# Node stages of a four-layer graph network: sums and inner rows in PSUM, GpSimd's additions behind VectorE's, another order of the slots

## What is computed

```
x = _layernorm(x + _L0_gnn_ref(x, ...))   # edge MLP, mean over a node's edges, node MLP, inner layernorm
x = _layernorm(x + _L1_gnn_ref(x, ...))   # attention with self loops, + x @ skip_W + biases, inner layernorm
x = _layernorm(x + _L2_gnn_ref(x, ...))   # attention, 8 heads' layout of 16 columns, no inner norm
x = _layernorm(x + _L3_gnn_ref(x, ...))   # attention, batch norm, relu, x + h
```

## Time and profile before

| | us |
|---|---|
| median of 3 runs | 8903.67 |
| lowest and highest run | 8887.96, 8942.08 |
| the profiled execution | 8913.7 |
| its span | 8911.7 |
| VectorE busy | 5056.9 |
| TensorE busy | 6934.7 |
| GpSimd busy | 6300.6 |

### The profile page before, as it was taken

One profiled execution on the slowest core, in us unless ns is written; L12 is line 12 of the kernel. 1 busy time (PEld: TensorE's weight loads), 2 busy tenths in 40 slices (PEclk: granted clock), 3 DMA queues, 4 the chain that ended last, 5 costly groups with the idle time before them and its releaser, 6 DMA issues.

```text
span 8911.7 us, 139091 instructions
## 1 busy us (share of the span) xinstructions
PE 6934.7 (78%) x41513; PEld 5837.6 (66%) x41514; DVE 5056.9 (57%) x12625; ACT 2080.3 (23%) x7255; POOL 6300.6 (71%) x6607
## 2 busy tenths in 40 slices
PE   6999999998777777777747777777766777777775
PEld 5777777776566666666636666666655666666664
DVE  3333333334766666666686666666666666666666
ACT  2222222222322222222222222222212222222222
POOL 4777777775677777777657777777765777777774
PEclk8999889998888888887768888888877888888886
DMA  3333333332222222222222222222222222222221
GB/s 100 80 78 80 76 76 77 80 78 64 73 66 66 66 66 66 67 67 66 64 70 69 69 69 69 68 70 69 69 64 66 68 69 69 68 70 69 69 69 49
DMA packets 425472, 625.66 MB, mean 70 GB/s; under 512 B 189634, under 2 KB 305617, under 8 KB 425293
## 3 DMA queue, kind: packets, MB, share of 16 engines
q0 software_dynamic: 206336, 462.61, 21.3%
q1 hardware_dynamic: 219086, 162.49, 7.1%
HBM read 598.03 MB, written 26.58 MB: 70 GB/s over the span
## 4 chain that ended last, share of the span: by engine, by line
PE 37%; POOL 26%; issue 17%; DVE 12%; DVEq 4%; DMA 2%; SPq 1%; ACT 1%; POOLq 0%; ACTq 0%
POOL G L559 25%; PE ps L708 11%; PE ps L755 8%; PE ps L730 6%; PE ps L725 6%; DVEq L1216 3%; DVE msg L1335 3%; PE ps L698 2%; DVE acc L1242 2%; DMA G<-rows,idx 2%; PE ps L776 1%; DVE acc L1232 1%; DVE shared L1289 1%; DVE shared L1297 1%; PE ps L786 1%
## 5 line engine op out<-in xcount | busy, mean ns | idle before, releaser
L559 POOL DMA_INDIRECT G<-rows,idx x6448 | 6127.0, 950 | 2197.1 <-issue 1914.3
L1162 DVE TENSOR_TENSOR memb<-rel,ps 128x1664 f32<-128x1664 f32 x496 | 936.3, 1888 | 1828.2 <-PE ps L708 1827.9
L708 PE MATMUL ps<-msg,memb 128*128 128x136 f32 (+2 forms) x12896 | 1733.7, 295 | 128.0 <-DVE msg L1335 125.5
L755 PE MATMUL ps<-membT,shared 128*104 128x128 f32 x9672 | 1772.0, 356 | 2.2 <-ACT membT L919 2.2
L708 PEld LDWEIGHTS ps<-msg,memb 128*128 128x128 f32 x12896 | 1655.6, 203 | 156.2 <-issue 87.7
L755 PEld LDWEIGHTS ps<-membT,shared 128*104 128x104 f32 x9672 | 1605.5, 236 | 24.7 <-issue 3.0
L698 PE MATMUL ps<-ident,memb 128*128 128x128 f32 x6448 | 1092.9, 312 | 462.6 <-DVE memb L1162 420.6
L1242 DVE TENSOR_TENSOR acc<-acc,ps 128x136 f32 (+2 forms) x3472 | 1023.8, 295 | 421.4 <-DVE acc L1242 346.3
L698 PEld LDWEIGHTS ps<-ident,memb 128*128 128x128 f32 x6448 | 792.5, 155 | 679.8 <-issue 362.9
L919 ACT ACTIVATE membT<-ps 128x512 f32<-128x512 f32 x1984 | 952.2, 504 | 77.6 <-PE ps L698 66.5
L1335 DVE TENSOR_TENSOR msg<-G,ps 128x1768 f32<-128x1768 f32 x372 | 742.7, 1996 | 242.6 <-PE ps L786 238.5
(11 more groups left out here) (179 smaller groups left out, 4627.6 us busy)
## 6 DMA issues: line engine op xcount, KB each, us to landing
G<-rows,idx POOLq DMA_INDIRECT x6448
shared<-marks_all SPq DMA_DIRECT2D x372, 156.0 KB
shared<-in_edge_attr SPq DMA_DIRECT2D x124, 256.0 KB
shared<-in_edge_attr SPq DMA_DIRECT2D x124, 160.0 KB
rows<-msg SPq DMA_DIRECT2D x36, 288.0 KB, 2.8
idx<-in_src SPq DMA_DIRECT2D x496, 6.5 KB
xrows<-msg SPq DMA_DIRECT2D x24, 256.0 KB, 2.2
memb<-xrows SPq DMA_DIRECT2D x24, 256.0 KB, 3.0
```

Source lines behind the costliest of these rows:

```text
L559: nc.gpsimd.indirect_dma_start(G[:, b, t, 0:rows[l].shape[1]], None, rows[l], bass.IndirectOffsetOnAxis(idx[:, b, t:t + 1], 0)).then_inc(g ...
L708: last = mm(ps_sum[k // 2][:, 0:width], memb[:, b, k * P:(k + 1) * P], msg[:, b, k, 0:width], start=k % 2 == 0, stop=k % 2 == 1 or k == K - 1)
L755: last = mm(ps_sc[b][0:JH, :], adz[:, k // 2, K - 1 - k:K - 1 - k + JH], membT[:, k, :], start=k == 0, stop=False)
L1162: tt(memb[:, b, :].rearrange("p (k n) -> p k n", k=K), r, w, ALU.is_equal).then_inc(memb_ready, 1)
```

## The change

- PSUM banks are used in the node stages for three things: the weighed sums of stages 1 and 2 (`n_weighed`, banks 0 and 1), the inner rows (`n_y_rows`, banks 6 and 7) and, in the last loop, the relu rows (`f_relu_rows`, banks 4 and 5). `s_y` is gone.
- `addends` is split. `base_rows(t+1)` stands between `power(1, t-1)` and `power(0, t)`; `residual_rows(t+1)` stands after them and waits, for blocks from 2 on, for `n_agg`, the sums of block t+2.
- In stage 1 the row of biases `reps[3]` is added by TensorE (four more matmuls a block with one-row weights) and not by GpSimd; the own rows times their shares remain on GpSimd.
- In stage 0 the bias product `b2_u1` of the hidden rows comes last of the three.
- In stage 2 VectorE's slot is another: residual, table of block t-2, shifts of block t, sums of block t+1.

```diff
-        s_r, s_y, s_t = (ring(gflat, 2 * k * BLK, 2) for k in range(3))
+        s_r, s_t = (ring(gflat, 2 * k * BLK, 2) for k in range(2))
+        n_weighed, n_y_rows, f_relu_rows = ps[:, 0:2, :], ps[:, 6:8, :], ps[:, 4:6, :]
...
-            def addends(l, s):
+            def base_rows(l, s):
                 pool.wait_ge(x_in[x], 16 * (ring_uses(g, 3) + 1))
                 if s >= 2:
                     pool.wait_ge(n_var[0], g - 1)
...
-                    nc.gpsimd.tensor_tensor(base, base, rep(3), ALU.add).then_inc(n_base, 1)
+
+            def residual_rows(l, s):
+                g = NS * l + s
+                n, x = QN[s], g % 3
+                if s >= 2:
+                    pool.wait_ge(n_agg, NS * l + min(s + 2, NS))
                 if s >= 3:
                     pool.wait_ge(n_var[1], g - 2)
-                nc.gpsimd.tensor_tensor(xb, xr, rep(4 + l), ALU.add).then_inc(n_xb, 1)
+                nc.gpsimd.tensor_tensor(rowsof(s_xb[:, x, 0:n * P]), rowsof(s_x[:, x, 0:n * P]),
+                                        reps[:, 4 + l, :].unsqueeze(1).to_broadcast([P, n, P]), ALU.add).then_inc(n_xb, 1)
...
                 mm(n_hidden[:, 0:n], u1[:, 0, :], xT[:, d], start=True, stop=False)
+                pe.wait_ge(n_aggT_in, s + 1)
+                mm(n_hidden[:, 0:n], w2u[:, :], s_agg[:, s % 2, 0:n], start=False, stop=False)
                 if s == 0:
                     pe.wait_ge(n_some_row, 32)
-                mm(n_hidden[:, 0:n], b2_u1[0:1, :], some_row[0:1, d], start=False, stop=False)
-                pe.wait_ge(n_aggT_in, s + 1)
-                mm(n_hidden[:, 0:n], w2u[:, :], s_agg[:, s % 2, 0:n], start=False, stop=True).then_inc(n_hid_out, 1)
+                mm(n_hidden[:, 0:n], b2_u1[0:1, :], some_row[0:1, d], start=False, stop=True).then_inc(n_hid_out, 1)
...
-                        last = mm(n_update[:, f], xT[:, s * BLK + q * P:s * BLK + (q + 1) * P], wsk[:, :],
-                                  start=True, stop=True)
+                        mm(n_update[:, f], xT[:, s * BLK + q * P:s * BLK + (q + 1) * P], wsk[:, :],
+                           start=True, stop=False)
+                        last = mm(n_update[:, f], ones[0:1, :], reps[0:1, 3, :], start=False, stop=True)
...
-                normalise(s_y[:, g % 2, :], s_r[:, g % 2, :], 0, g % 2, QN[s], n_y)
+                normalise(n_y_rows[:, g % 2, :], s_r[:, g % 2, :], 0, g % 2, QN[s], n_y)
...
-                then(weighed(both_halves(s, 0, MW), shares(1, s)))
+                g = NS + s
+                weighed(both_halves(s, 0, MW), shares(1, s), wide(n_weighed[:, g % 2, 0:QN[s] * P], QN[s])).then_inc(n_agg, 1)
...
-                    then(tt(wide(d, n), wide(d, n), of_heads(even(s, 0, MW)), ALU.add))
+                    dve.wait_ge(n_agg, g + 1)
+                    then(tt(d, d, n_weighed[:, r, 0:n * P], ALU.add))
...
-                if s >= 2:
-                    dve.wait_ge(n_xnew, g - 1)
-                then(weighed(both_halves(s, 0, MW), weights_of(s), wide(s_t[:, g % 2, 0:QN[s] * P], QN[s])))
+                weighed(both_halves(s, 0, MW), weights_of(s), wide(n_weighed[:, g % 2, 0:QN[s] * P], QN[s])).then_inc(n_agg, 1)
...
-                    stt(s_t[:, s % 2, 0:n], xT[:, cols_of(s)], 2.0, s_y[:, s % 2, 0:n], ALU.mult,
+                    stt(s_t[:, s % 2, 0:n], xT[:, cols_of(s)], 2.0, f_relu_rows[:, s % 2, 0:n], ALU.mult,
```

More of the change, by code:

```diff
@@ L583, in addends @@
                 if l == 0:
-                    nc.gpsimd.tensor_tensor(base, xr, rep(2), ALU.add).then_inc(n_base, 1)
+                    nc.gpsimd.tensor_tensor(rowsof(s_base[:, g % 2, 0:n * P]), rowsof(s_x[:, x, 0:n * P]),
+                                            reps[:, 2, :].unsqueeze(1).to_broadcast([P, n, P]), ALU.add).then_inc(n_base, 1)
                 else:
@@ L608, in node_stage @@
                 for t in SLOTS:
[L609 to L615, removed]
+                    s = at(t, 1)
+                    if s is not None and l < 2:
+                        power(1, l, s)
+                    s = at(t, -1)
+                    if s is not None and l < 2:
+                        base_rows(l, s)
                     s = at(t, 0)
                     if s is not None:
-                        power(1, l, s)
+                        power(0 if l < 2 else 1, l, s)
+                    s = at(t, -1)
+                    if s is not None and l < 2:
+                        residual_rows(l, s)
             for l in range(4):
@@ L1524, in node_stage @@
                     s = at(t, 0)
[L1525 to L1538 removed]
+                    g = NS * l + t
+                    if l < 2:
+                        if s is not None:
+                            update(l, s)
+                        s = at(t, 1)
+                        if s is not None:
+                            shifts(1, (g - 1) % 2, QN[s], n_rstd[1], g, n_shift[1])
+                        s = at(t, 3)
+                        if s is not None:
+                            table(l, s)
+                        s = at(t, 0)
+                        if s is not None:
+                            shifts(0, g % 2, QN[s], n_rstd[0], g + 1, n_shift[0])
+                        s = at(t, -2)
+                        if s is not None:
+                            (means, shared_sums)[l](s)
+                        s = at(t, 0)
+                        if s is not None:
+                            residual(l, s)
+                    else:
+                        if s is not None:
+                            residual(l, s)
+                        s = at(t, 2)
+                        if s is not None:
+                            table(l, s)
+                        s = at(t, 0)
+                        if s is not None:
+                            shifts(1, g % 2, QN[s], n_rstd[1], g + 1, n_shift[1])
                         s = at(t, -1)
@@ L1541, in node_stage @@
                             value_sums(s)
-                    else:
-                        s = at(t, -2)
-                        if s is not None:
-                            (means, shared_sums)[l](s)
-                    s = at(t, 0)
-                    if s is not None:
-                        residual(l, s)
             for l in range(4):
```

46 lines of the change are left out of this document (12 added, 34 removed).

## The result

| | before | after |
|---|---|---|
| median of 9 runs each, us | 8923.5 | 8847.7 |
| lowest and highest run, us | 8888.0, 8942.1 | 8817.1, 8879.8 |
| ratio, 95% interval | | 0.9928, 0.991 to 0.9946 |
| the profiled execution, us | 8913.7 | 8858.5 |

The change saves 76 us: 0.85% between the medians, 0.7% by the ratio, whose interval excludes no change. The median of the nine runs of before stands 20 us above that of the first three, on which the forecast was built, so its difference (73 us) is the better measure of it than its level (8831).

The account below looks back on a forecast made before the run. GpSimd's gathers fill the untouched sweeps; VectorE's queue bounds stages 0 and 1, a round trip stage 2. Gains 22.3 + 27.8 + 21 + 1.5 = 73 us, from 8903.7 to 8831 us, range 8797 to 8877.

Parts of the forecast that it names:

- The level: Whole kernel: 8831 us after the change, against 8903.7, the median of the first three runs.
- The stop of two SBUF inputs against a GpSimd addition: Stages 0 and 1: each waits for the other's end, costing 1.06 + 0.97 us per slot of stage 0.
- Stage 0: First node stage: 22.3 us less, with slots of 8.6 us and a start 2.0 us earlier.
- Stage 1: Second node stage: 27.8 us less, slots falling from 12.00 to 9.2 us.
- The bias on TensorE: Stage 1: four more one-row matmuls a block, at most 2.08 us more, costed at 0 because covered.
- Stage 2: Third node stage: 21 us less, slots falling from 7.41 to 5.65 us.
- PSUM as an operand: All node stages: about 104 VectorE passes read or write PSUM, at 0 us extra each.
- slower: Rival, chance 0.03: PSUM makes VectorE's passes longer; 0.7 us more on each of 104 cancels the gain.
- The last loop: After the last sweep: power falls from 1.39 to 1.01 us; 1.5 us gained (0 to 4.5).
- One input is held too: Rival, chance 0.07: GpSimd additions also hold VectorE passes with one SBUF input; 30 us gained, kernel at 8874.
- TensorE bounds stage 0: Rival, chance 0.12: TensorE's 7.7 us per slot grow at a lower clock; kernel at 8843 or 8869.
- More: Rival, chance 0.10: TensorE's clock grant rises and stages' last slots shrink, some 5 us a stage; 8816.

Follow-up runs that it names:

- e1: Changed kernel with the inner rows of stages 0 and 1 and stage 2's sums back in SBUF: slots of 9.47, 10.18 and 5.72 us.
- e2: Kernel before, its orders kept, with inner rows and stage 2's sums in PSUM, those sums without their wait: stages of 152.1, 174.3 and 89.0 us.
- e3: Changed kernel without the residual addition's wait for the sums: slots of 9.4 to 9.8 us in stage 0, 10.17 in stage 1.
- e6: Changed kernel with all GpSimd additions of stages 0 and 1 behind the sums: stages of 128.8, 143.5 and 81.9 us; ratio to before 0.9911.
- e4: Changed kernel with stage 1's bias on GpSimd again and stage 0's hidden products in old order: slots of 9.72 us in stage 1, 8.52 in stage 0.
- e5: Changed kernel with stage 1's sums and the last loop's rows in SBUF, stage 2's table a slot later: slots 9.12 and 5.73, stage 2 85.2 us.
- e7: The changed kernel unaltered, run once more: ratio to before 0.99; stages of 129.4, 146.1 and 83.3 us, 82.5 behind the last sweep.

## Why the prediction was right, point by point

**The whole.** Forecast: 73 us less. Measured: 73.9 in the edited parts, 76 between the medians. The parts were off by up to 1.7 us, and these errors cancelled in the sum. The level, 8831, was 17 us low, about as much as the median of the first three runs of before lay below that of all nine (20).

**The stop of two SBUF inputs against a GpSimd addition.** This was the core, and e1, e2 and e3 show it from three sides: a stop of 0.95 to 1.06 us appears when either the operand or the place is put back. The rule of the Trainium skill's page "SBUF — State Buffer", section "Who interferes with whom", fits: of the passes of 128x512 with one SBUF input, 47 ran beside a GpSimd addition or multiplication in stages 0 and 1 of after, and all took 0.69 to 0.70 us.

**Stage 0: 22.3 forecast, 20.6 measured.** The full slots gave 1.96 us each (1.9 forecast); the 0.2 us for the small pass held by the base addition was forecast at 0.13, and e6 took it back. The start gave 2.3 (2.0 forecast). TensorE's last hidden product has only this left behind the wait of the earlier trace rows:

```profile
2196.83 1.92 PE L816 MATMUL ps<-shared,w2u 128*128 128x512 f32 x2
2201.22 1.12 PE L819 MATMUL ps<-shared,b_u 1*128 1x512 f32 x2 [2.48 <-DMA shared<-flags]
```

Two terms were mis-sized. Slot 10 gave 0.9 and not 2.0: its short sums no longer cover ScalarE's inner rows, the very thing that I took off in stage 1's slot 10 and forgot here.

```profile
2296.91 0.70 DVE L1485 TENSOR_TENSOR ps<-ps,reps 128x512 f32<-128x512 f32 x1 [0.93 <-ACT ps L1000]
```

And the end, from the last update on, took 12.6 us instead of 11.1. There TensorE's products follow one another with nothing to hide them, and eight of L854 took 1.30 us in before at 2306.42, at 2.4 GHz, but 2.39 in after, at 1.2 GHz. The change isn't shown to be the cause: e2, with the orders of before, has 2.39 and an end of 12.4 too, and e3, with those of after, 1.30 and 11.3.

```profile
2314.39 2.39 PE L854 MATMUL ps<-wext,xT 128*128 128x152 f32 x8 [0.69 <-ACT xT L919]
```

**Stage 1: 27.8 forecast, 29.1 measured.** Slots of 9.11 (9.2 forecast); the full ones gave 2.89 each, slot 0 1.1 (0.6), slot 10 1.8 (1.9). The bias on TensorE, costed at 0, cost 0, but its price was mis-sized. I had put it at "at most 2.08 more" for an update. At the same granted clock of 0.50 the eight products of before took 2.08 us and the sixteen of after 5.86, which is 3.78 more:

```profile
4528.53 0.80 PE L832 MATMUL ps<-wsk,xT 128*128 128x128 f32 x2 [2.62 <-DVE varn L1370]
...
4533.60 0.79 PE L834 MATMUL ps<-reps,ones 1*128 1x128 f32 x2
...
4534.66 0.69 DVE L1471 TENSOR_TENSOR G<-ps,memb 128x512 f32<-128x512 f32 x1
```

They end 0.26 us before the update that reads them. So it is, within 0.01, in seven of slots 1 to 9; in the other two the clock was higher and 2.5 us are left. Slot 10 leaves 0.14. TensorE was busy for 105 us of 146, 8.1 a slot and not 7.3 (60 of 175 in before), though in ten full slots it still sat idle for 22 us waiting for VectorE. So the 0 held by a narrow margin, and by luck as far as the argument goes; a slot of stage 1 much shorter than 9.11 would meet TensorE at this clock. That the row on TensorE was necessary (0.61 a slot, e4) wasn't in the sum; I had counted only the stops that it removed.

**Stage 2: 21 forecast, 21.1 measured, by other parts.** Slots of 5.73 against 5.65, and the full slots gave 1.7 each, ten of them where I had counted eleven. I overlooked that before the change made two blocks' sums ahead of the first residual and after makes one: the first residual comes 2.1 us earlier, and those sums fall into slot 10, which gave only 0.46 us. The stage's end gave 1.8; I had put the earlier table at 0.7, and e5 gives 3.0 for it at the same clock. The errors cancelled, which is luck. And the cause was half misread: PSUM for stage 2's sums, which I made a part of the gain, is worth nothing once the order is changed (e1), because by then ScalarE has long read `s_t`.

**PSUM as an operand: 0 forecast.** L1485, in place in PSUM, 0.69; L1487 0.69; L1446 writing into PSUM 0.70 against 0.69 into SBUF. None of these passes took even 1.1 times its former length, so the rival "slower" had nothing to stand on. The 65 ns a pass that the Trainium skill's page "VectorE: DVE Perf Modes", section "The TRN2 errata", would give for a source in PSUM are not in the traces.

**The last loop: 1.5 forecast, 3.1 measured.** The power takes 1.01 there (1.39 before); some 0.25 us of the 0.38 came through in each of twelve blocks.

**The rivals.** "One input is held too": L1485 and L1487 beside a full addition show no stop. "TensorE bounds stage 0": in after it still waits for VectorE in each slot, at a granted clock of 0.79 for the stage:

```profile
2252.42 1.12 PE L819 MATMUL ps<-shared,b_u 1*128 1x512 f32 x2
2254.61 0.66 PE L806 MATMUL ps<-ident,acc 128*128 128x128 f32 x4 [1.07 <-DVE acc L1457]
```

In e7 it came close. There every second slot of the later ones took 8.74 us, and at the end of each of these VectorE waited 0.15 us for TensorE's update product, the sign that the prediction had named for this rival:

```profile
2237.67 0.69 DVE L1471 TENSOR_TENSOR G<-ps,memb 128x512 f32<-128x512 f32 x1 [0.15 <-PE ps L830]
```

The slots between them took 8.32, so that the mean stayed at 8.53. "More": the clock's grant didn't rise (0.79, 0.54 and 0.57 against 0.77, 0.57 and 0.58 between the same bounds), and the ends of stages 0 (after against before) and 2 (e7 against after) took 1.5 us more where eight products ran at 1.2 GHz. The sweeps, which the argument left out, moved by 17 us, over three times the errors of its four parts added up without their signs (4.7).

## What to carry to other kernels

Look for small VectorE passes that take about as long as a GpSimd instruction beside them: here a 0.16 us pass took 1.22. Such a stop needs both an operand and a place: in stage 0 moving the second operand to PSUM gave nothing, moving the GpSimd work half, the two together all, so each addition was put behind a semaphore at the place where VectorE reads PSUM. Compare stages and slots rather than whole times when a change is under 1%: single executions of the same sweep code differed by 50 us in the first sweep alone, while nearly all full slots of stages 1 and 2 repeated within 0.03 us. Those of stage 0 varied by 0.4 us, though their mean stayed at 8.5.

## What the runs showed of the hardware

A small pass with one SBUF input can be held as well: L1370 (one input of 128x4, two constants) takes 0.17 us, 0.37 where a GpSimd addition still runs, and 0.78 in e4; in each case it ends with the addition. Row statistics with one input beside the same additions keep their 0.87 and 0.38 us. The Trainium skill's page "SBUF — State Buffer", section "Who interferes with whom", names this kind of operation (`tensor_scalar`) as one that can take the shared ports; the traces agree.

Matmuls with one-row weights were not cheap. A pair of them took 0.79 us in stage 1 at a granted clock of 0.50, as much as a pair with weights of 128 rows (0.80), and sixteen of the two kinds in turn took 5.86 us, 0.37 each, where the eight of before, all of one kind, took 2.08, 0.26 each. Why the mixed ones stand further apart isn't shown.

On the chip of e1 to e4 GpSimd's gathers took no longer to issue, 949 ns each, but the engine sat idle for 6423 us between them instead of 2219, and VectorE's pass that reads the gathered rows was idle before it for 1931 us instead of 783. The page of e1, the gathers and the pass that reads them:

```profile
L561 POOL DMA_INDIRECT G<-rows,idx x6448 | 6120.1, 949 | 6423.1 <-DVE msg L1335 3113.5
...
L1255 DVE TENSOR_TENSOR msg<-G,ps 128x512 f32<-128x512 f32 x496 | 288.1, 587 | 1931.2 <-remote 1177.6
```

DMA moved 48 GB/s there and 71 in the profile of after. That the rows landed later is the reading of these figures; what made them late on that chip stays open. Slots of stages that an experiment left as they were had the same length on both chips: 8.52 and 5.73 in e4 and in after.
